# Expert stage of a ViT block: token features by a transposing DMA in place of row loads, TensorE transposes and ScalarE copies

## The reference

```python
flat = layernorm(h).reshape(-1, 192)
probs = softmax(flat @ router_w.T)                  # 8 experts
top_w, top_i = top_k(probs, 2); top_w = top_w / top_w.sum(-1, keepdims=True)
for e in range(8):
    w_e = sum(top_w * (top_i == e), -1)[:, None]
    hid = gelu(flat @ w1[e] + b1[e], approximate=False)   # 192 -> 768
    out = out + w_e * (hid @ w2[e] + b2[e])               # 768 -> 192
h = h + out
```

## Time and profile before

| | us |
|---|---|
| median of 3 runs (1689.94 to 1693.35) | 1693.18 |
| profiled execution, its time | 1697.55 |
| its span | 1695.8 |
| TensorE busy | 1491.4 (88%) |
| VectorE busy | 1121.2 (66%) |
| GpSimd busy | 861.2 (51%) |
| ScalarE busy | 718.4 (42%) |

### The profile page before, as it was taken

How to read it: one execution, slowest core, us unless ns; L and a number is a source line. 1 busy time by engine, 2 the same in 40 slices (tenths; PEclk the granted TensorE clock), 3 DMA queues, 4 the chain that set the end, 5 groups by cost and what they waited for, 6 DMA issues and landing times. The chain is left out here.

```text
span 1695.8 us, 52298 instructions
## 1 busy us (share of the span) xinstructions
PE 1491.4 (88%) x18345; PEld 1238.1 (73%) x18346; DVE 1121.2 (66%) x2875; ACT 718.4 (42%) x1201; POOL 861.2 (51%) x900
## 2 busy tenths in 40 slices
PE   4777999999999999899562799999999999999995
PEld 4666888888888788788451577777777777777774
DVE  3466777778777776777645466666666666666663
ACT  2443444444444444444421444444444444444441
POOL 3122656656555555555535155545554555455544
PEclk9887999999999999999865799999999999999998
DMA  6654555555555555555422334443444334433432
GB/s 206 205 172 126 157 148 154 153 151 155 144 150 154 150 152 145 143 139 150 113 76 95 93 59 60 60 65 57 59 60 65 57 59 60 65 58 59 59 45 29
DMA packets 190164, 182.64 MB, mean 108 GB/s; under 512 B 86361, under 2 KB 166437, under 8 KB 188989
## 3 DMA queue, kind: packets, MB, share of 16 engines
q1 hardware_dynamic: 125834, 111.46, 23.7%
q0 software_dynamic: 41680, 41.84, 16.8%
q10 hardware_dynamic: 22499, 27.28, 4.9%
HBM read 104.93 MB, written 65.29 MB: 100 GB/s over the span
## 5 line engine op out<-in xcount | busy, mean ns | idle before, releaser
L988 POOL DMA_INDIRECT out<-y,token x219 | 368.5, 1683 | 73.7 <-issue 72.9
L1096 PE MATMUL down<-w_hi,g_hi 128*128 x1314 | 323.7, 246 | 1.9 <-DVE y L1062 1.1
L1098 PE MATMUL down<-w_hi,g_lo 128*128 x1314 | 323.0, 246 | 0.0
L1097 PE MATMUL down<-w_lo,g_hi 128*128 x1314 | 322.9, 246 | 0.0
L1084 PE MATMUL up<-e_xT,w_hi 128*128 128x384 f16 x1314 | 286.7, 327 | 0.0
L1009 ACT ACTIVATE act_out<-up,bias 128x384 f32<-128x384 f32 x438 | 250.9, 581 | 73.3 <-PE up L1084 73.2
L391 POOL DMA_INDIRECT sorted_scratch<-payload,place x212 | 219.5, 1035 | 59.9 <-issue 56.9
L775 PE MATMUL near<-we,patches 128*120 128x192 f32 x1272 | 226.2, 335 | 17.4 <-DMA patches<-in_xt 10.0
L1001 ACT COPY e_xT<-turned 128x1152 f16<-128x1152 f16 x73 | 81.6, 1118 | 353.8 <-PE turned L1076 353.8
L775 PEld LDWEIGHTS near<-we,patches 128*120 128x120 f32 x1272 | 210.2, 187 | 27.8 <-issue 27.7
L1045 DVE TENSOR_TENSOR g_lo<-act_out,g_hi 128x768 f16<-128x768 f32 x219 | 209.9, 958 | 7.6
(11 more groups left out here) (154 smaller groups left out, 2745.9 us busy)
## 6 DMA issues: line engine op xcount, KB each, us to landing
patches<-in_xt SPq DMA_DIRECT2D x53, 720.0 KB
rows<-sorted_scratch SPq DMA_DIRECT2D x73, 301.5 KB, 2.8
v_diag<-v_scratch SPq DMA_DIRECT2D x159, 89.2 KB
v_scratch<-v_rows SPq DMA_DIRECT2D x53, 191.2 KB, 3.0
tab<-tab_scratch SPq DMA_DIRECT2D x53, 180.0 KB
out<-h ACTq DMA_DIRECT2D x52, 180.0 KB
stage<-in_w ACTq DMA_DIRECT2D x8, 1152.0 KB
k_diag<-qk SPq DMA_DIRECT2D x424, 15.8 KB
```

Source lines behind the costliest of these rows:

```text
L988: pool.indirect_dma_start(out=out, out_offset=bass.IndirectOffsetOnAxis(ap=token[k][:, n:n + 1], axis=0), in_=y[k % 2][:, n, :], in_offset ...
L1096: pe.matmul(dst, g_hi[k % 2][:, m, cols], high, start=(m == 0), stop=False)
L1097: pe.matmul(dst, g_hi[k % 2][:, m, cols], low, start=False, stop=False)
L1098: ins = pe.matmul(dst, g_lo[k % 2][:, m, cols], high, start=False, stop=(m == MF - 1))
```

## The change

The rows of a batch are no longer loaded whole. One transposing DMA (`transpose=True`) reads the 384 feature words of 384 rows and writes them into `xT[k]` with features on the partitions and rows along them, [128, 3, 384]. A second DMA loads the other 18 words (36 bytes) of each row into a smaller `rows[k]`, now with row 128r + p on partition p, the order of the transposed columns. Each has a semaphore of its own. `turn` and `take` are gone with their semaphores and the two PSUM banks; `xT` has four buffers, and `up` has UPS = 4 banks, numbered through by (MF * k + m) % UPS, so an up product waits for the gelu four before. SyncE waits for the up products of the buffer's last batch in place of its transposes. Which 128 tokens go with one scatter changes with the row order.

```diff
 
 BATCH = 384
 PARTS = BATCH // 128
+UPS = 4
 REGION = TOKENS + BATCH
 SPARE = EXPERTS * REGION
 BATCHES = (CHOSEN * TOKENS + EXPERTS * (BATCH - 1)) // BATCH
@@ -921,23 +922,23 @@
         def sem(name):
             return ctx.enter_context(nc.semaphore(name))
 
-        rows = [sb(f"rows{k}", [128, PARTS, PAYLOAD], U16) for k in range(4)]
+        rows = [sb(f"rows{k}", [128, PARTS, PAYLOAD - NUMBER_AT], U16) for k in range(4)]
         token = [sb(f"token{k}", [128, PARTS], U32) for k in range(4)]
         weight = [sb(f"weight{k}", [128, PARTS], F32) for k in range(4)]
         b2s = sb("b2s", [128, EXPERTS, D], F32)
         bias2 = [sb(f"bias2_{k}", [128, D], F32) for k in range(4)]
         bias = [sb(f"bias{k}", [128, MF], F32) for k in range(2)]
-        xT = [sb(f"e_xT{k}", [128, PARTS, 3, 128], F16) for k in range(2)]
+        xT = [sb(f"e_xT{k}", [128, 3, BATCH], F16) for k in range(4)]
         act_out = sb("act_out", [128, MF, BATCH], F32)
         g_hi = [sb(f"g_hi{k}", [128, MF, BATCH], F16) for k in range(2)]
         g_lo = [sb(f"g_lo{k}", [128, MF, BATCH], F16) for k in range(2)]
         y = [sb(f"y{k}", [128, PARTS, D], F32) for k in range(2)]
         carrier = sb("e_carrier", [32, 2], F32)
-        up = [pb(f"up{k}", [128, BATCH], F32) for k in range(3)]
+        up = [pb(f"up{k}", [128, BATCH], F32) for k in range(UPS)]
         down = pb("down", [128, PARTS, 512], F32)
-        turned = pb("turned", [128, 2, 512], F32)
-        s = {n: sem("e_" + n) for n in "turned xT_set up_done gelu_done hi_done lo_done down_done y_set biased meta_set memory carried b2_in".split()}
+        s = {n: sem("e_" + n) for n in "up_done gelu_done hi_done lo_done down_done y_set biased meta_set memory carried b2_in".split()}
         s_rows = [sem(f"e_rows{k}") for k in range(4)]
+        s_xT = [sem(f"e_xT_in{k}") for k in range(4)]
         s_sent = [sem(f"e_sent{k}") for k in range(2)]
         SENT = 16 * PARTS
         block = ctx.enter_context(nc.Block())
@@ -957,7 +958,8 @@
             def load(u, k):
                 at = batch_row[0:1, u:u + 1] if isinstance(u, int) else batch_row[0:1, bass.ds(u, 1)]
                 row = sp.value_load(at, min_val=0, max_val=SPARE)
-                sp.dma_start(rows[k][:], sorted_dram[bass.ds(row, BATCH), :].rearrange("(p r) c -> p r c", r=PARTS))\
+                sp.dma_start(xT[k][:], sorted_dram[bass.ds(row, BATCH), 0:NUMBER_AT].bitcast(F16), transpose=True).then_inc(s_xT[k], 16)
+                sp.dma_start(rows[k][:], sorted_dram[bass.ds(row, BATCH), NUMBER_AT:PAYLOAD].rearrange("(r p) c -> p r c", r=PARTS))\
                   .then_inc(s_rows[k], 16)
 
             load(0, 0)
@@ -967,7 +969,7 @@
             def body(u, k, p):
                 if not last(u, 1):
 
-                    need(sp, s["turned"], u - 1)
+                    need(sp, s["up_done"], MF * (u - 1))
                     need(sp, s["meta_set"], u - 1)
                     load(u + 2, (k + 2) % 4)
 
@@ -994,28 +996,17 @@
 
         @block.scalar
         def _(act):
-            def take(u, k):
-
-                act.wait_ge(s["turned"], u + 1)
-                need(act, s["up_done"], MF * (u - 1))
-                act.copy(xT[k % 2][:].rearrange("p n c r -> p (n c r)"), turned[:].rearrange("p b n -> p (b n)").bitcast(F16)[:, 0:3 * BATCH])\
-                   .then_inc(s["xT_set"], 1)
-
             def gelu(u, k):
                 act.wait_ge(s["meta_set"], u + 1)
                 for m in range(MF):
                     act.wait_ge(s["up_done"], MF * u + m + 1)
                     need(act, s["lo_done"], MF // 2 * (u - 1) + m // 2 + 1)
-                    act.activation(act_out[:, m, :], up[m % 3][:], ACT.Gelu, bias=bias[k % 2][:, m:m + 1], scale=1.0 / WS)\
+                    act.activation(act_out[:, m, :], up[(MF * k + m) % UPS][:], ACT.Gelu, bias=bias[k % 2][:, m:m + 1], scale=1.0 / WS)\
                        .then_inc(s["gelu_done"], 1)
 
-            take(0, 0)
-            take(1, 1)
             gelu(0, 0)
 
             def body(u, k, p):
-                if not last(u, 1):
-                    take(u + 2, k + 2)
                 if not last(u):
                     gelu(u + 1, k + 1)
 
@@ -1030,9 +1021,9 @@
                 need(dve, s["gelu_done"], MF * (u - 1))
                 dve.tensor_scalar(bias[k % 2][:], b1s[:, bass.ds(e, 1), :].rearrange("p a m -> p (a m)"), 0.0, None, ALU.add)
                 dve.tensor_scalar(bias2[k][:], b2s[:, bass.ds(e, 1), :].rearrange("p a d -> p (a d)"), WS, None, ALU.mult)
-                dve.tensor_scalar(weight[k][:], rows[k][:, :, WEIGHT_AT:PAYLOAD].bitcast(F32)[:, :, bass.ds(e, 1)].rearrange("p n a -> p (n a)"),
+                dve.tensor_scalar(weight[k][:], rows[k][:, :, WEIGHT_AT - NUMBER_AT:].bitcast(F32)[:, :, bass.ds(e, 1)].rearrange("p n a -> p (n a)"),
                                   0.0, None, ALU.add)
-                dve.tensor_copy(token[k][:], rows[k][:, :, NUMBER_AT:WEIGHT_AT].bitcast(U32).rearrange("p n a -> p (n a)"))\
+                dve.tensor_copy(token[k][:], rows[k][:, :, 0:WEIGHT_AT - NUMBER_AT].bitcast(U32).rearrange("p n a -> p (n a)"))\
                    .then_inc(s["meta_set"], 1)
 
             def split(u, k):
@@ -1067,22 +1058,13 @@
 
         @block.tensor
         def _(pe):
-            def turn(u, k, p):
-                rows_in(pe, k, p)
-                need(pe, s["xT_set"], u)
-                for n in range(PARTS):
-                    for c in range(3):
-                        bank, at = (3 * n + c) // 8, (3 * n + c) % 8 * 128
-                        ins = pe.transpose(turned[:, bank, :].bitcast(F16)[:, at:at + 128], rows[k][:, n, 128 * c:128 * c + 128].bitcast(F16), ident16[:])
-                ins.then_inc(s["turned"], 1)
-
-            def up_product(u, k, e):
-                pe.wait_ge(s["xT_set"], u + 1)
+            def up_product(u, k, p, e):
+                pe.wait_ge(s_xT[k], 16 * (p + 1))
                 for m in range(MF):
-                    need(pe, s["gelu_done"], MF * u + m - 2)
+                    need(pe, s["gelu_done"], MF * u + m - UPS + 1)
                     for j, (c, w, h) in enumerate(PRODUCTS):
-                        ins = pe.matmul(up[m % 3][:], w1s[h][:, bass.ds(e, 1), w, 128 * m:128 * m + 128].rearrange("p a c -> p (a c)"),
-                                        xT[k % 2][:, :, c, :], start=(j == 0), stop=(j == len(PRODUCTS) - 1))
+                        ins = pe.matmul(up[(MF * k + m) % UPS][:], w1s[h][:, bass.ds(e, 1), w, 128 * m:128 * m + 128].rearrange("p a c -> p (a c)"),
+                                        xT[k][:, c, :], start=(j == 0), stop=(j == len(PRODUCTS) - 1))
                     ins.then_inc(s["up_done"], 1)
 
             def down_product(u, k, e):
@@ -1098,15 +1080,11 @@
                         ins = pe.matmul(dst, g_lo[k % 2][:, m, cols], high, start=False, stop=(m == MF - 1))
                 ins.then_inc(s["down_done"], 1)
 
-            turn(0, 0, 0)
-            turn(1, 1, 0)
-            up_product(0, 0, expert_of(pe, 0))
+            up_product(0, 0, 0, expert_of(pe, 0))
 
             def body(u, k, p):
-                if not last(u, 1):
-                    turn(u + 2, (k + 2) % 4, p + (k + 2) // 4)
                 if not last(u):
-                    up_product(u + 1, k + 1, expert_of(pe, u + 1))
+                    up_product(u + 1, (k + 1) % 4, p + (k + 1) // 4, expert_of(pe, u + 1))
                 down_product(u, k, expert_of(pe, u))
 
             batch_pipeline(pe, body)
```

## The result

The changed kernel takes 1648.3 us (median of 4 runs, 1646.99 to 1649.56) against 1691.6 us before: ratio 0.9744, 95% interval 0.9727 to 0.9761, or 40 to 46 us less. The forecast was 1657.7 us, 35.5 less, so the direction and the bound held and the size was too small. The measured time lies 0.3 us inside the lower end of the forecast's range, 1648 to 1696.

What follows compares the result with a forecast made beforehand. The prediction took TensorE's instruction stream to bound the expert stage; -36.5 us from the transposes and +1 us at the start made -35.5, so 1693.2 became 1657.7 us, range 1648 to 1696 (likeliest case 1648 to 1667).

Steps and rivals of the forecast that it cites:

- Part 1: TensorE's transposes leave the expert stage: a batch falls from 9.99 to 9.47 us, 36.5 us less in all, bounds 33 and 39.
- Part 2: ScalarE's 73 feature copies of 1118 ns go; they lie beside TensorE's work, so nothing is gained.
- Part 3: A fourth bank for the up products gives nothing, as three suffice: up product 0.81 us, gelu 581 ns.
- Part 4: TensorE's read of the expert number ahead of the up products stays hidden: nothing, at most 0.5 us a batch.
- Part 5: The transposing load takes about 3 us of the DMA engines, bounds 1.13 and 3.3, and stays hidden in the 9.47 us batch.
- Part 6: At the expert stage's start, removed transposes and copy against low clock and later bias table: +1 us, bounds -2 and +4.
- Rival B: The transposing load's blocks go one behind the other and bound the batch at 15.0 us: about 2049 us, chance 15%.
- Rival C: GpSimd's scatters, delayed by loads, become the bound: 1800 us, chance 5%, or 1684 us with half a load ahead, 6%.
- Rival D: No gain: TensorE's sequencer reads the expert number too late, 0.5 us of stall replacing the transposes each batch: 1692 us, chance 5%.

## Why the prediction was right, and where its size was off

- **What bounds it.** Right. TensorE's stream sets the stage before and after.
- **Part 1, transposes.** The term itself was right: 0.50 us in most batches (9.83 against 9.33 with the transposes back). The new batch of 9.47 us was not, and this is the step that was off. I read it in the last batches of before and called it free of gaps; it held 0.12 us of stall at the entry to down, inside the 4.57 us of the down products. 54 products at the chain's step of some 0.0825 us are 4.45, and I could have worked that out, or read it ahead of the loop, where before takes 9.83 - 0.50 = 9.33. Two errors met here. The transposes gave less than I took, 0.44 us a batch or 71 x 0.44 = 31 us and not 36.5, since the loop's gap grew from some 0.1 to 0.37 us every fourth batch when they went. And the stall that I let stay went too, 0.13 us a batch, some 9 us, of which the next point has a part.
- **Part 2, copies.** Right: 0.01 us.
- **Part 3, fourth bank.** Wrong. I compared the gelu's duration with the up product's and found three banks enough for the data; they are. But the fourth takes away a stall behind the up products: 0.065 us a batch, 4.6 us. By the waits it stands where the expert's number is read; that the bank lets the sequencer queue the last product and read sooner is the likely way, and the queue itself is in no row. Part 1 named this stall, and let it "get looser", without giving the bank its price.
- **Part 4, the read for up.** Right: no gap ahead of up. The gap that is left stands once in four batches ahead of down.
- **Part 5, loads.** Right that they are hidden, and the size was inside its bounds: 1.7 us of the engines between 1.13 and 3.3, nearer to the lower end than my 3. By bytes that is 294912 / 1.7 us = 173 GB/s, against 308736 / 1.13 = 273 for the plain load. So the rule of the Trainium skill ("Advanced Engine Details and Errata", X-Bar Transpose (TRN2)) that transposing DMAs are as fast as regular ones, at 350 to 400 GB/s, does not hold for this shape, and it did not matter.
- **Part 6, the start.** I took +1 us, within -2 to +4. From the first load's issue to the second up product it was 953.22 - 939.29 = 13.93 before and 943.35 - 929.56 = 13.79 after. The parts were right, removed work against a bias table that comes later; they cancel.
- **Rival B** did not happen. The price in the Trainium skill ("VectorE: DVE Perf Modes", The three transpose paths), 1309 ns a block by DMA, would make nine blocks 11.8 us; here nine land in 4.1 us, and a fourfold load still keeps pace. So it can't be multiplied by the blocks; no run here loads a single one. **Rival C** is visible as GpSimd's five waits, and 49 with doubled loads, and never reached TensorE; the room is larger than the 1.3 us that I counted, and which of the buffers gives it was not tried. **Rival D** did not happen as stated, 0.5 us in each batch, but a small piece of it did: the wider gap once in four batches, some 0.06 us in the mean.
- **The sum and the range.** The stage gave 40.3 us. My terms reach that only at their far ends, 39 from part 1 and 2 from part 6, and then for other reasons than the real ones. The lower end of 1648 does not follow from them either: 1693.2 - 41 = 1652. That the measured 1648.3 still falls inside the range is luck, as is that the two errors of part 1 partly cancel. The median before was moreover 1691.6 us and not the 1693.2 that I started from. What the medians have beyond the stage, some 3 us, no profile places; the spread of the attention part is wider than that.

## What to carry to other kernels

When an engine's stream is the bound, count its stream time from the instruction's own step (54 x 0.0825 us) and compare it with the length read from the trace. What is left over is a stall with a cause of its own, and a change may remove it or move it. Work that goes from a full engine can also uncover a gap that it had hidden, as the loop's here. A buffer that the data does not need can still take away a stall, here of 0.065 us a batch. A transposing DMA was a good trade for transposes on a full TensorE, issued some 30 us ahead of its use; order the first loads by who needs them first.

## What the runs showed of the hardware

- A transposing DMA of 384 x 384 two-byte values took at most 1.7 us of the sixteen DMA engines and 4.1 us from issue to landing, where the plain load of as many bytes took 1.13 and 2.8. Its issue holds SyncE for 1.33 us, a plain one 0.34.
- Where TensorE's sequencer reads one value from SBUF into a register, its stream lost nothing behind the down products (steps of 0.08 us). Behind the up products (steps of 0.16 us) it lost 0.12 us in the loop with three banks, and nothing ahead of the loop, or with four banks in three of four batches. In the middle of the up products it lost 0.16 us.
- Going round the loop of four batches cost TensorE's stream 0.37 us where no transposes stood in it, some 0.1 us where they did, and nothing when the loop was written out.
- A scatter instruction on GpSimd takes 1.56 us, and often about 2.05 when it lies beside VectorE's splits.
